# Matrix products of one tile shape put side by side, and the empty rows of the last expert unit left out, in a fused attention and mixture-of-experts kernel

## The chip, the cores and the metric

The kernel runs on 1 core of one Trainium2 chip. The metric is the device time in microseconds, the median of three runs.

## The reference

Eight images of 64 x 64 x 3 and eight texts of 77 tokens of width 64 go through one layer of three parts. In short:

```python
patches = x -> (8, 64 tokens, 192)                  # 8 x 8 patches
t  = ln(ln(patches) @ W1 + b1)                      # to width 64
t  = concat([t, t, t], tokens)                      # three copies: 192 tokens
q  = silu(ln(t @ Wp1 + bp1)) @ Wp2 + bp2
h  = concat([q, txt], tokens)                       # 192 + 77 = 269 tokens
# attention: a linear recurrence over the tokens, state S of 64 x 64 per batch element
r, k, v, w, a, g = ...                              # projections of x and of the shifted x
S  = S * exp(w_t) + (S @ -kk_t) (kk_t a_t)' + v_t k_t' ;  o_t = S @ r_t
h1 = h + (groupnorm(o) + bonus) * g @ W_o
# experts: 8 of them, the best 2 of each token, hidden width 128
c  = softmax over the top 2 of (ln(h1) @ Wg + bg), 0 elsewhere
y  = h1 + sum_e c_e * (relu(ln(h1) @ W1[e] + b1[e]) @ W2[e] + b2[e])
```

## The kernel before

Tokens are cut into chunks of 32. A tile of 128 rows holds 32 tokens of four batch elements (J = 4), and two such groups (G = 2) make the eight. 192 image tokens are 6 chunks, but the three copies share their work, so that there are 6 units to prepare (NU = 6): unit 0 (the first image chunk at the very beginning), 1 and 2 (image), and 3 to 5 (text). Unit 5 (LAST) holds 13 real tokens and 19 empty ones.

**Stages.** First the patches are normalised and projected (`image(i, a)`, two halves a, six sub-steps i). Then the units are prepared in three rounds r with two slots s each (`SLOTS = ((4, 0), (1, 2), (3, 5))`): `proj`, `lora`, `cum`, `hats`, `gates`, `products`, `keep`, `turn`, `apply`, four levels of a doubling inverse (`lt(r, li, s)` and `tlt(r, li, s)`), `out`, `fuse`. `step(k)` and `read(k)` carry the state over the nine chunks. `stats` to `parts` are the norms and the choice of experts, once for each of three groups of three chunks. The expert part has six units of 384 columns (half a group): `front(u, p)` does experts 2p and 2p + 1 (W1 as two rounded parts, L1640 and L1641, and the gate spread over 128 rows, L1652), ScalarE takes the relu (L938) and VectorE multiplies by the gate (L1314). `back(u, p)` adds the same two experts' W2 products (L1674, F32, 64 columns of the array each, the even expert's in rows 0 to 63 of the output and the odd one's in rows 64 to 127), and p = 3 also the b2 term (L1677). ScalarE then copies YS (L947), `fold(u)` adds the two halves of the rows on PE (L1686), VectorE adds the result to H1 (L1328), and SyncE stores it.

**Order.** One function `run` lists all steps. Each engine runs the same list, with its own part of each step (or nothing), in that order; semaphores connect the parts. So a step's place in the list is its place in the queue of all engines that have a part in it.

**Names.** `bank(s, i)` is a PSUM bank of slot s. An F32 product leaves two records in the trace, one in F32R (L1640, L1641, L1652, L1677) one. `residue` is GpSimd's W1l = W1 - W1h (L678), which waits for ScalarE's rounding of W1h in `factors`; `blank` is eight small and two larger memsets on GpSimd (L686 to L690); `remain` is two small subtractions there. The steps on PE, by their lines: `image(0)` L1372, `proj` L1411 (128 x 128), L1414 (128 x 64), L1415 (128 x 128); `cum` L1433 (128 x 128) and L1435 (128 x 64); `products` L1456 (64 x 128); `apply` L1474, L1476 (128 x 128), L1478 (128 x 64), for one g after the other; `lt` L1490; `tlt` L1502, L1506; `out` L1515; `fuse` L1527, L1532 (128 x 64), L1535 (128 x 128); `step` L1557; `read` L1571 (128 x 32).

**Waits that matter below.** `hidden(0)`, the first product of the experts, waits for both `hoc_ready` and `t_ready` of all units, which ScalarE's and VectorE's parts of `fuse(2, 0)` and `fuse(2, 1)` raise. `weights(i, h)` transposes the gate coefficients CP, which VectorE's `parts(i)` completes; ScalarE copies them to CT, on which `spread` waits (`ctc_ready`).

Of the kernel before, what the change touches and what calls it, by code (L numbers as in the profile page):

```python
# [19 lines left out]
F32 = mybir.dt.float32  # L20
# [91 lines left out]
def build(nc, patches, text, consts, pick, rows, cols, tokw, attw, w1, w2, out):  # L112
    ctx = ExitStack()
    with ctx:
# [110 lines left out]
        XHL = [sb(f"XHL{i}", [P, Q, P], F32R) for i in range(GROUPS)]  # L225
        CF = sb("CF", [P, GROUPS * Q, E])
# [17 lines left out]
        CP = sb("CP", [P, Q, 2, E])  # L244
# [105 lines left out]

        NX = E * NU
# [16 lines left out]
        def run(patch=skip, words=skip, even=skip, lift=skip, texts=skip, small=skip, mixes=skip, residue=skip,  # L368
# [48 lines left out]
            lt(0, 2, 0)  # L417
# [3 lines left out]
            tlt(0, 2, 0)  # L421
            keep(0, 1)
            lora(1, 0)
            turn(0, 1)
            lt(0, 3, 0)
            lt(0, 0, 1)
            cum(1, 0)
            tlt(0, 3, 0)
            apply(0, 1)
            out(0, 0)  # L430
            hats(1, 0)
            tlt(0, 0, 1)
            lt(0, 1, 1)
            fuse(0, 0)
            tlt(0, 1, 1)
            proj(1, 1)
            lt(0, 2, 1)
            products(1, 0)
            tlt(0, 2, 1)
            lt(0, 3, 1)  # L440
            keep(1, 0)
            lora(1, 1)
            turn(1, 0)
            tlt(0, 3, 1)
            lt(1, 0, 0)
            gates(1, 0)
            out(0, 1)
            cum(1, 1)
            apply(1, 0)
            fuse(0, 1)  # L450
            tlt(1, 0, 0)
            hats(1, 1)
            gates(1, 1)
            lt(1, 1, 0)
            proj(2, 0)
            products(1, 1)
            tlt(1, 1, 0)
            lt(1, 2, 0)
            lora(2, 0)
            tlt(1, 2, 0)  # L460
            turn(1, 1)
            keep(1, 1)
            cum(2, 0)
            lt(1, 3, 0)
            lt(1, 0, 1)
            apply(1, 1)
            hats(2, 0)
            tlt(1, 3, 0)
            tlt(1, 0, 1)
            lt(1, 1, 1)  # L470
            out(1, 0)
            tlt(1, 1, 1)
            lt(1, 2, 1)
            fuse(1, 0)
# [7 lines left out]
            products(2, 0)  # L482
            keep(2, 0)
            read(1)
            fuse(1, 1)
            turn(2, 0)
            lora(2, 1)
            apply(2, 0)
            step(2)
            cum(2, 1)  # L490
            read(2)
            lt(2, 0, 0)
            step(3)
            stats(0)
            tlt(2, 0, 0)
            read(3)
            centre(0)
            lt(2, 1, 0)
            step(4)
            tlt(2, 1, 0)  # L500
            hats(2, 1)
            gates(2, 1)
            lt(2, 2, 0)
# [3 lines left out]
            tlt(2, 2, 0)  # L507
            keep(2, 1)
            read(5)
# [3 lines left out]
            stats(1)  # L513
            centre(1)
            lt(2, 3, 0)
            lt(2, 0, 1)
            att(0)
            tlt(2, 3, 0)
            tlt(2, 0, 1)
            lt(2, 1, 1)  # L520
            tlt(2, 1, 1)
# [1239 lines left out]
```

## Time and profile before

| | |
|---|---|
| median of 3 runs | 215.8 us (214.55 to 216.31) |
| the profiled execution | 215.78 us, its span 214.0 us |
| mean granted clock | 0.932 of 2.4 GHz |
| busy, of the span | PE 184.4 us (86%), VectorE 149.3 (70%), ScalarE 86.9 (41%), GpSimd 75.6 (35%) |
| instructions | PE 1259, VectorE 539, ScalarE 222, GpSimd 131 |

PE is TensorE's products and PEld its weight loads; DVE is VectorE, ACT ScalarE, POOL GpSimd. Ends of PE's records are modelled and records overlap, so a difference between two starts tells more than a duration. "x4" is four records merged into one row; what stands in brackets is the idle time before a row and what ended it. Of the time outside the span, 1.8 us, the profile shows nothing.

### The profile page before, as it was taken

To read this page: it belongs to the slowest core of one execution; us is meant where nothing else is said; L and a number is where in the kernel's file an instruction comes from. 1 tells how busy PE (TensorE), PEld (TensorE's weight loads), DVE (VectorE), ACT (ScalarE), POOL (GpSimd) and SP (SyncE) were. 2 spreads that over 40 slices of the span, in tenths; PEclk is the share of its full clock that TensorE was granted. 3 is DMA by queue.
4 is the path that set the end of the run, shared out by engine and by line. 5 is a ranking of instruction groups with operands and counts; after the bars stand their busy time and mean duration, and the time that the engine had idled before them with its cause. 6 is when DMAs were issued, how large, how long until landed. Compare 5 with 4: busy or idle time off the path is not lost. (4 is left out here: it accounts for less than half of the span.)

```text
span 214.0 us, 3831 instructions
## 1 busy us (share of the span) xinstructions
PE 184.4 (86%) x1259; PEld 138.9 (65%) x1259; DVE 149.3 (70%) x539; ACT 86.9 (41%) x222; POOL 75.6 (35%) x131
## 2 busy tenths in 40 slices
PE   0584564998999999999999899976899999999994
PEld 0461552586776877977768777854578667866762
DVE  2997658756853884733676989879865978876550
ACT  2062012264454435544323224443464625748440
POOL 3916529653623746514661603273000202000000
PEclk9988555699999999999999999999699999999998
DMA  6920000000000000000000000000000000000000
GB/s 186 335 84 2 0 0 0 0 5 0 2 2 3 0 0 3 0 0 3 0 5 0 0 3 0 2 3 0 0 2 3 0 23 18 0 18 3 18 18 18
DMA packets 2498, 4.06 MB, mean 19 GB/s; under 512 B 416, under 2 KB 1824, under 8 KB 2480
## 3 DMA queue, kind: packets, MB, share of 16 engines
q1 hardware_dynamic: 1872, 3.05, 4.4%
q10 hardware_dynamic: 608, 0.77, 1.1%
q8 instruction: 10, 0.16, 0.3%
q14 instruction: 8, 0.07, 0.1%
HBM read 3.24 MB, written 0.59 MB: 18 GB/s over the span
## 5 line engine op out<-in xcount | busy, mean ns | idle before, releaser
L1171 DVE TENSOR_TENSOR YI<-PS,KC 128x256 f32<-128x256 f32 x24 | 9.8, 419 | 13.1 <-PE PS L1490 12.8
L1640 PE MATMUL PS<-XHL,W1h 128*128 128x384 f32 x48 | 18.4, 383 | 0.0
L783 POOL TENSOR_SCALAR ve<-mv 128x6 f32<-128x6 f32 x6 | 1.5, 258 | 45.3 <-DVE mv L1220 45.3
L1652 PE MATMUL PS<-CT,PK 128*128 128x384 f32 x48 | 16.6, 347 | 0.4 <-ACT CT L929 0.4
L1641 PE MATMUL PS<-XHL,W1l 128*128 128x384 f32 x48 | 16.7, 348 | 0.0
L938 ACT ACTIVATE xT<-PS,CL 128x384 f32<-128x384 f32 x24 | 13.1, 579 | 7.9 <-PE PS L1641 7.7
L1490 PE MATMUL PS<-PI,AT 128*128 128x128 f32 x96 | 15.7, 289 | 0.5 <-DVE BL L1165 0.2
L1506 PE MATMUL PS<-QT,YI 128*128 128x128 f32 x96 | 14.8, 277 | 0.0
L1490 PEld LDWEIGHTS PS<-PI,AT 128*128 128x128 f32 x96 | 12.5, 190 | 2.6 <-ACT PI L883 1.7
L938 ACT ACTIVATE FAB<-PS,CL 128x384 f32<-128x384 f32 x24 | 13.0, 581 | 2.1 <-PE PS L1641 2.1
L1502 PE MATMUL PS<-YI,QT 128*128 128x128 f32 x72 | 12.0, 289 | 1.8 <-DVE YI L1171 1.8
L883 ACT COPY PI<-PS 128x256 f32<-128x256 f32 x18 | 6.7, 373 | 16.6 <-PE PS L1502 16.4
L1506 PEld LDWEIGHTS PS<-QT,YI 128*128 128x128 f32 x96 | 12.7, 192 | 0.1
L1502 PEld LDWEIGHTS PS<-YI,QT 128*128 128x128 f32 x72 | 9.4, 191 | 3.4 <-issue 3.4
L1640 PEld LDWEIGHTS PS<-XHL,W1h 128*128 128x128 f32 x48 | 9.4, 196 | 2.8 <-issue 1.8
L886 ACT COPY QT<-PS 128x256 f32<-128x256 f32 x24 | 8.9, 372 | 3.0 <-PE PS L1506 1.6
L1652 PEld LDWEIGHTS PS<-CT,PK 128*128 128x128 f32 x48 | 9.3, 193 | 0.9 <-issue 0.9
L1342 PE MATMUL PS<-KC,P 128*128 128x128 f32 x13 | 3.4, 334 | 7.4 <-DVE P L974 7.1
L709 POOL TENSOR_TENSOR BL<-BP,KC 128x256 f32<-128x256 f32 x12 | 8.7, 744 | 2.1 <-DVE BP L1126 2.1
L1641 PEld LDWEIGHTS PS<-XHL,W1l 128*128 128x128 f32 x48 | 9.4, 195 | 0.0
L709 POOL TENSOR_TENSOR LKT<-PI,KC 128x256 f32<-128x256 f32 x10 | 7.4, 762 | 5.4 <-ACT PI L895 5.4
L1674 PE MATMUL PS<-HC,W 128*64 128x384 f32 x48 | 9.3, 501 | 0.0
(216 smaller groups left out, 488.2 us busy)
## 6 DMA issues: line engine op xcount, KB each, us to landing
KC<-in_consts SPq DMA_DIRECT2D x1, 706.0 KB, 7.4
out_h<-H SPq DMA_DIRECT2D x6, 96.0 KB, 1.6
ARCH<-in_w SPq DMA_DIRECT2D x1, 512.0 KB, 9.1
AW<-in_attw SPq DMA_DIRECT2D x1, 484.0 KB, 8.3
PT<-in_patches SPq DMA_DIRECT2D x2, 192.0 KB, 3.3
RW<-in_rows ACTq DMA_DIRECT2D x1, 296.0 KB, 5.1
W<-in_w SPq DMA_DIRECT2D x1, 256.0 KB, 9.2
HT<-in_text ACTq DMA_DIRECT2D x1, 192.0 KB, 3.3
```

Source lines behind the costliest of these rows:

```text
L709: return nc.gpsimd.tensor_tensor(dst, src.to_broadcast([P, J, D]), const("block").rearrange("p (j d) -> p j d", j=J), ALU.mult)
L883: copy(PI[s][:, :, :].rearrange("p g t -> p (g t)"), bank(s, 2)[:, 0:G * P])\
L886: copy(QT[s][:, :, :].rearrange("p g t -> p (g t)"), bank(s, 1)[:, 0:G * P]).then_inc(q_ready[s], 1)
L938: nc.scalar.activation(RL[x % len(RL)], PS[:, Z_BANK[x % 2], 0:HALF * P], ACT.Relu, bias=CL[:, COLS["b1e"]][:, e:e + 1]).then_inc(relu_don ...
L1171: TT(YI[s][:, :, :], pairs(bank(s, 2)[:, 0:G * P]), twice(const(f"m{LEVELS[li]}")), ALU.mult)\
L1490: last = mm(bank(s, 2)[:, g * P:(g + 1) * P], AT[s][:, g, :], PI[s][:, g, :], start=True, stop=True)
L1502: last = mm(bank(s, 2)[:, g * P:(g + 1) * P], QT[s][:, g, :], YI[s][:, g, :], start=True, stop=True)
L1506: last = mm(bank(s, 1)[:, g * P:(g + 1) * P], YI[s][:, g, :], QT[s][:, g, :], start=True, stop=True)
L1640: mm(z, W1h[:, e * EH:(e + 1) * EH], xhl, start=True, stop=False)
L1641: mm(z, W1l[:, e * EH:(e + 1) * EH], xhl, start=False, stop=True).then_inc(z_ready, 1)
L1652: mm(PS[:, C_BANK[x % 2], 0:HALF * P], PK[:, e * P:(e + 1) * P], gates_of(u), start=True, stop=True).then_inc(c_ready, 1)
L1674: mm(PS[(e % 2) * D:(e % 2 + 1) * D, Y_BANK, 0:HALF * P], W2[:, e * D:(e + 1) * D], HC[e], start=e < 2, stop=False).then_inc(y_done, 1)
```

## The change

1. `proj`: the product with Wlora's first block writes all 128 columns (64 of A_w and 64 more, which nobody reads) instead of 64. `cum`: the two products per group with `seq` become one with both groups. `apply`: the products with KP (128 x 64) of both groups stand behind the full-width products of both groups.
2. `weights`: CP is 128 wide with zeros behind its 16 coefficients, so its transposes write all 128 rows, and the memsets of CT fall away.
3. The last expert unit (FINAL = 5) has 232 columns: 128 of a full chunk and 2 x 4 x 13 of the last one. `dense` copies its features (XD5) and gates in that form, and its YS is spread again by two copies.
4. `out(2, 1)`, of unit 5 with its 13 tokens, waits for the third level; the fourth, `lt(2, 3, 1)` and `tlt(2, 3, 1)`, leaves the list.
5. The list of `run` gets another order throughout. It has the same steps but for the two of point 4.

```diff
+        FINAL, TAIL = 2 * GROUPS - 1, TXT - (NTXT - 1) * C
+        COUNT = [HALF * P] * FINAL + [P + 2 * J * TAIL]
...
             patch(0)
             patch(1)
             words()
+            texts()
             even(0)
             even(1)
-            texts()
-            lift(0)
-            lift(1)
             small()
             mixes()
             clear()
             factors()
+            lift(0)
+            lift(1)
+            residue()
+            proj(0, 0)
             image(0, 0)
             image(0, 1)
-            proj(0, 0)
-            remain()
-            residue()
+            lora(0, 0)
             image(1, 0)
             image(1, 1)
             image(2, 0)
-            lora(0, 0)
             image(2, 1)
+            blank()
+            cum(0, 0)
+            remain()
             image(3, 0)
             image(3, 1)
             image(4, 0)
-            blank()
-            cum(0, 0)
             image(4, 1)
             hats(0, 0)
             gates(0, 0)
@@ -404,74 +408,74 @@
             products(0, 0)
             keep(0, 0)
             proj(0, 1)
+            apply(0, 0)
             turn(0, 0)
-            apply(0, 0)
             image(5, 1)
+            lora(0, 1)
             lt(0, 0, 0)
-            lora(0, 1)
+            cum(0, 1)
             tlt(0, 0, 0)
-            cum(0, 1)
             lt(0, 1, 0)
...
             heads(1)
             split(0)
-            lt(2, 2, 1)
+            lt(2, 1, 1)
             att(1)
-            tlt(2, 2, 1)
-            lt(2, 3, 1)
+            tlt(2, 1, 1)
             out(2, 0)
             rest(0)
+            lt(2, 2, 1)
             feat(0, 0)
-            tlt(2, 3, 1)
+            tlt(2, 2, 1)
             feat(0, 1)
             split(1)
+            out(2, 1)
             rest(1)
-            out(2, 1)
             rank(0)
-            fuse(2, 0)
             choose(0)
             feat(1, 0)
             feat(1, 1)
+            parts(0)
+            fuse(2, 0)
             fuse(2, 1)
-            parts(0)
             rank(1)
             weights(0, 0)
             front(0, 0)
             weights(0, 1)
+            front(0, 1)
             choose(1)
             parts(1)
-            front(0, 1)
+            back(0, 0)
+            front(0, 2)
             weights(1, 0)
-            front(0, 2)
+            front(0, 3)
             weights(1, 1)
-            front(0, 3)
+            back(0, 1)
             step(6)
-            back(0, 0)
-            back(0, 1)
             back(0, 2)
             read(6)
...
             front(5, 1)
+            back(4, 3)
             front(5, 2)
-            back(4, 3)
+            back(5, 0)
             front(5, 3)
             fold(4)
             tail()
-            back(5, 0)
             back(5, 1)
             back(5, 2)
             back(5, 3)
...
             def clear():
                 nc.gpsimd.memset(PK[:, :].bitcast(F32), 0.0)
-                for s in range(2):
-                    last = nc.gpsimd.memset(CT[s][:, :].bitcast(F32), 0.0)
-                last.then_inc(zeros, 1)
+                nc.gpsimd.memset(CP[:, :, 2:, :], 0.0).then_inc(zeros, 1)
...
+            def dense(dst, src, u):
+
+                if u < FINAL:
+                    return copy(dst, src)
+                copy(dst[:, 0:P], src[:, 0:P])
+                return copy(dst[:, P:COUNT[u]].rearrange("p (q c) -> p q c", c=TAIL),
+                            src[:, P:].rearrange("p (q c) -> p q c", c=C)[:, :, 0:TAIL])
...
+                src = PS[:, FFN_BANK[i], 0:HALF * P]
+                last = copy(XHL[i][:, h * HALF:(h + 1) * HALF, :].rearrange("p q t -> p (q t)"), src)
+                if 2 * i + h == FINAL:
+                    last = dense(XD5[:, :], src, FINAL)
...
-                mm(wide(r, s)[0:D, 0:G * P], Wlora[:, 0:D], x, start=True, stop=True)
+                mm(wide(r, s)[:, 0:G * P], Wlora[:, 0:P], x, start=True, stop=True)
...
                 for i, m in enumerate((masks[:, P:2 * P], masks[:, 0:P], const("suffix"))):
                     mm(bank(s, 0)[:, i * P:(i + 1) * P], m, lw, start=True, stop=True)
-                for g in range(G):
-                    last = mm(bank(s, 0)[g * D:(g + 1) * D, 3 * P:3 * P + J], LW[s][:, g, :], const("seq"),
-                              start=True, stop=True)
-                last.then_inc(cum_ready, 1)
+                mm(bank(s, 0)[:, 3 * P:3 * P + J], lw, const("seq"), start=True, stop=True).then_inc(cum_ready, 1)
...
                        start=True, stop=True)
                     mm(bank(s, 1)[:, P + g * D:P + (g + 1) * D], LKT[s][:, g, 1, :], RK[s][:, g, 2, :],
                        start=True, stop=True)
+                for g in range(G):
                     last = mm(bank(s, 1)[g * D:(g + 1) * D, 2 * P:4 * P], KP[s][:, g, :],
                               VB[s][:, g, :, :].rearrange("p j d -> p (j d)"), start=True, stop=True)
                 last.then_inc(lvov_ready, 1)
...
-                pe.wait_ge(q_ready[s], level(r, 4, 5))
+                pe.wait_ge(q_ready[s], level(r, 3 if SLOTS[r][s] == LAST else 4, 5))
...
-                xhl = XHL[u // 2][:, u % 2 * HALF:(u % 2 + 1) * HALF, :].rearrange("p q t -> p (q t)")
-                z = PS[:, Z_BANK[x % 2], 0:HALF * P]
+                xhl = XD5[:, :] if u == FINAL else XHL[u // 2][:, u % 2 * HALF:(u % 2 + 1) * HALF, :].rearrange("p q t -> p (q t)")
+                z = PS[:, Z_BANK[x % 2], 0:COUNT[u]]
...
```

## Rows read from the trace of the kernel before

**Rows 1.** Windows: stage, its length, busy us and instructions by engine, clock, DMA.

```profile
0.00:42.00 42.00, 23.31 (x91) 16.16 (x91) 29.77 (x120) 9.46 (x25) 24.39 (x53) 0.72 0.23 77
42.00:105.00 63.00, 61.76 (x433) 48.57 (x433) 39.33 (x136) 29.62 (x87) 29.80 (x50) 1.00 0.01 1
105.00:151.00 46.00, 40.09 (x359) 31.84 (x358) 37.67 (x161) 15.15 (x42) 18.19 (x25) 1.00 0.01 1
151.00:155.00 4.00, 3.63 (x14) 2.62 (x12) 3.46 (x12) 2.40 (x7) 0.00 (x0) 0.58 0.00 0
155.00:206.50 51.50, 51.12 (x345) 37.50 (x344) 37.54 (x111) 29.70 (x61) 3.17 (x4) 1.00 0.03 9
```

**Rows 2.** Chain that ended last: start, duration, what (us).

```profile
197.60 2.09 PE PS L1674 x12
199.68 0.37 PE PS L1640
200.06 0.17 PE PS L1641
...
203.94 0.80 PE PS L1674 x4
```

**Rows 3.** PE timeline (start, duration): apply(0, 1), and a fuse of both groups.

```profile
59.96 0.33 PE L1474 MATMUL PS<-RK,LKT 128*128 128x64 f32 x2
...
60.45 0.65 PE L1478 MATMUL PS<-VB,KP 128*64 128x256 f32 x2
61.02 0.43 PE L1474 MATMUL PS<-RK,LKT 128*128 128x64 f32 x2
...
62.19 0.71 PE L1515 MATMUL PS<-LVHA,QT 128*128 128x128 f32 x4
...
65.62 0.60 PE L1532 MATMUL PS<-LKT,BP 128*64 128x256 f32 x4
66.16 0.66 PE L1535 MATMUL PS<-PI,BL 128*128 128x64 f32 x4
```

**Rows 4.** PE timeline: a proj and the step behind it.

```profile
51.59 1.03 PE L1411 MATMUL PS<-Wproj,XT 128*128 128x256 f32 x4
52.55 0.65 PE L1414 MATMUL PS<-XT,Wlora 128*64 128x256 f32 x2
...
53.76 1.13 PE L1456 MATMUL PS<-FAB 64*128 64x256 f32 x8
```

**Rows 5.** PE timeline: the end of cum(1, 1).

```profile
76.55 0.28 PE L1435 MATMUL PS<-KC,LW 128*64 128x4 f32 x4
76.77 0.43 PE L1474 MATMUL PS<-RK,LKT 128*128 128x64 f32 x2
```

**Rows 6.** PE timeline: lt(2, 3, 1) and the step behind it.

```profile
138.14 0.71 PE L1490 MATMUL PS<-PI,AT 128*128 128x128 f32 x4
138.69 0.61 PE L1515 MATMUL PS<-LVHA,QT 128*128 128x128 f32 x4
```

**Rows 7.** PE timeline: the wait ahead of the first weights transposes.

```profile
150.39 0.50 PE L1342 MATMUL PS<-KC,CP 128*16 128x128 f32 x3 [1.95 <-DVE CP L1306]
```

**Rows 8.** Timeline of all engines: two of ScalarE's activations.

```profile
201.99 1.11 ACT L938 ACTIVATE FAB<-PS,CL 128x384 f32<-128x384 f32 x2 [0.61 <-PE PS L1641]
```

**Rows 9.** Timeline of all engines: the cold start.

```profile
11.50 2.00 PE L1372 MATMUL PS<-TW,xT 96*128 96x64 f32 x16
...
14.35 2.04 PE L1411 MATMUL PS<-Wproj,XT 128*128 128x256 f32 x4 [0.85 <-DVE Wproj L1036]
...
19.39 2.84 DVE L974 TENSOR_SCALAR P<-P,mv,rs 128x64 f32<-128x64 f32 x2
...
19.84 2.33 POOL L678 TENSOR_TENSOR W1l<-ARCH,W1h 128x1024 fp32r<-128x1024 f32 x1
...
32.80 1.06 POOL L686 MEMSET ARCH<- 64x256 f32 x4
...
33.80 0.73 POOL L687 MEMSET ARCH<- 64x768 f32 x1
```

More of the change, by code:

```diff
@@ L225, in build @@
         XHL = [sb(f"XHL{i}", [P, Q, P], F32R) for i in range(GROUPS)]
+        XD5 = sb("XD5", [P, P + 2 * J * (TXT - (NTXT - 1) * C)], F32R)
         CF = sb("CF", [P, GROUPS * Q, E])
@@ L243, in build @@
         RC = sb("RC", [P, Q, 1])
[L244 removed]
+        CP = sb("CP", [P, Q, P // E, E])
         CT = two("CT", [P, Q * P], F32R)
@@ L420, in run @@
             products(0, 1)
-            tlt(0, 2, 0)
-            keep(0, 1)
+            lt(0, 2, 0)
             lora(1, 0)
             turn(0, 1)
+            keep(0, 1)
+            tlt(0, 2, 0)
+            cum(1, 0)
             lt(0, 3, 0)
+            apply(0, 1)
+            tlt(0, 3, 0)
             lt(0, 0, 1)
-            cum(1, 0)
-            tlt(0, 3, 0)
-            apply(0, 1)
             out(0, 0)
+            tlt(0, 0, 1)
             hats(1, 0)
-            tlt(0, 0, 1)
             lt(0, 1, 1)
             fuse(0, 0)
+            proj(1, 1)
+            products(1, 0)
             tlt(0, 1, 1)
-            proj(1, 1)
             lt(0, 2, 1)
-            products(1, 0)
-            tlt(0, 2, 1)
-            lt(0, 3, 1)
             keep(1, 0)
             lora(1, 1)
+            tlt(0, 2, 1)
+            gates(1, 0)
             turn(1, 0)
+            apply(1, 0)
+            lt(0, 3, 1)
+            proj(2, 0)
             tlt(0, 3, 1)
             lt(1, 0, 0)
-            gates(1, 0)
             out(0, 1)
+            tlt(1, 0, 0)
+            lt(1, 1, 0)
             cum(1, 1)
-            apply(1, 0)
             fuse(0, 1)
-            tlt(1, 0, 0)
+            tlt(1, 1, 0)
             hats(1, 1)
             gates(1, 1)
[L454 to L457, printed above, removed]
             lt(1, 2, 0)
             lora(2, 0)
+            products(1, 1)
+            keep(1, 1)
             tlt(1, 2, 0)
+            lt(1, 3, 0)
             turn(1, 1)
-            keep(1, 1)
             cum(2, 0)
-            lt(1, 3, 0)
+            apply(1, 1)
+            tlt(1, 3, 0)
             lt(1, 0, 1)
-            apply(1, 1)
+            out(1, 0)
+            tlt(1, 0, 1)
             hats(2, 0)
-            tlt(1, 3, 0)
-            tlt(1, 0, 1)
             lt(1, 1, 1)
-            out(1, 0)
+            fuse(1, 0)
             tlt(1, 1, 1)
             lt(1, 2, 1)
-            fuse(1, 0)
             tlt(1, 2, 1)
@@ L482, in run @@
             products(2, 0)
+            read(1)
             keep(2, 0)
-            read(1)
             fuse(1, 1)
-            turn(2, 0)
             lora(2, 1)
@@ L489, in run @@
             step(2)
+            turn(2, 0)
+            read(2)
             cum(2, 1)
-            read(2)
-            lt(2, 0, 0)
             step(3)
             stats(0)
+            lt(2, 0, 0)
+            read(3)
             tlt(2, 0, 0)
[L496 to L500, printed above, removed]
             hats(2, 1)
             gates(2, 1)
-            lt(2, 2, 0)
+            step(4)
+            lt(2, 1, 0)
+            centre(0)
             read(4)
@@ L506, in run @@
             step(5)
-            tlt(2, 2, 0)
             keep(2, 1)
+            tlt(2, 1, 0)
             read(5)
@@ L567, in run @@
             front(1, 3)
+            back(1, 0)
             centre(2)
-            back(1, 0)
             front(2, 0)
-            fold(0)
             back(1, 1)
@@ L591, in run @@
             rank(2)
-            choose(2)
+            fold(1)
             back(2, 3)
             front(3, 3)
-            parts(2)
-            fold(2)
             back(3, 0)
@@ L599, in run @@
             back(3, 2)
+            choose(2)
+            parts(2)
+            fold(2)
             weights(2, 0)
@@ L946, in back @@
                     act.wait_ge(fin_ready, u)
-                copy(YS[:, :], PS[:, Y_BANK, 0:HALF * P]).then_inc(ys_ready, 1)
+                if u < FINAL:
+                    last = copy(YS[:, :], PS[:, Y_BANK, 0:HALF * P])
+                else:
+                    copy(YS[:, 0:P], PS[:, Y_BANK, 0:P])
+                    last = copy(YS[:, P:].rearrange("p (q c) -> p q c", c=C)[:, :, 0:TAIL],
+                                PS[:, Y_BANK, P:COUNT[u]].rearrange("p (q c) -> p q c", c=TAIL))
+                last.then_inc(ys_ready, 1)
             run(texts=texts, factors=factors, image=image, proj=proj, lora=lora, cum=cum, hats=hats, turn=turn,
@@ L1617, in weights @@
                 else:
+                    pe.wait_ge(zeros, 1)
                     pe.wait_ge(cp_ready, i + 1)
                 for t in range(HALF):
-                    last = transpose(PS[0:2 * E, FFN_BANK[i], t * P:(t + 1) * P],
+                    last = transpose(PS[:, FFN_BANK[i], t * P:(t + 1) * P],
                                      CP[:, h * HALF + t, :, :].rearrange("p w e -> p (w e)"))
```

39 lines of the change are left out of this document (19 added, 20 removed).

## The prediction

> **What bounds the kernel now.** I read the busy table by stage first [rows 1]. It shows TensorE (PE) occupied for 61.76 of 63.0 us between 42 and 105, for 51.12 of 51.5 between 155 and 206.5, at the full clock in both, for 40.09 of 46.0 in between (VectorE, DVE: 37.67), and for only 23.31 of 42.0 in the first stage, where the granted clock averages 0.72 (most of it at 1.2 GHz) and DVE with 29.77 is the busiest engine. "Busy" overstates PE, since its records overlap, so the second view is the chain of work that ended last [rows 2]: from 172 us on, it is one PE product behind the other, with no waits worth naming until the last W2 product. PE takes its steps in one written order. Whatever is taken out of its stream in the two full stages comes off the end; in the first stage a latency chain rules; and between 105 and 151 PE and DVE take turns to be late. The third view is PE's timeline, in which the start of one step is subtracted from the start of the next, for a step's real price.
>
> **What a change of tile shape costs.** A visit of three W2 pairs (128 x 64 tiles) takes 2.08 us, from 197.60 to 199.68, and a visit of one pair 0.80 [rows 2]; so a pair is (2.08 - 0.80) / 2 = 0.64, and 0.16 stays per visit. The first 128 x 128 product behind it takes 0.37 instead of 0.17 to 0.18, 0.20 more [rows 2]. Together 0.36 us per visit, whatever its length. The Trainium skill (TensorEngine Tiling (Array Packing), Key Properties) says that a change of tiling mode drains TensorE, while a change of tile within the mode does not; the trace agrees in kind, and the page has no figure.
>
> **Part 1, apply (6 calls).** Now each group g goes 128 x 128, then 128 x 64: from 59.96 to 61.02 and on to 62.19, 2.23 us [rows 3]. Changed, the narrow products of both groups stand together. The full-width ones cost 0.49 for g = 0 up to the narrow product (59.96 to 60.45) and about 0.44 more for g = 1 without a second entry. The four narrow records write two different halves of the array's columns, as the four of L1532 do, which took 0.54 from 65.62 to 66.16 [rows 3]; with 0.06 for entering cold weights I take 0.60. Sum 1.53, saving 0.70 per call, 4.2 in all: 2.8 before 105, 1.4 behind. The bounds: 0.25 a call, if only the round trip between shapes goes and the two groups don't overlap; 0.75 if they do so perfectly.
>
> **Part 2, proj (6) and cum (6).** Wlora's first product becomes 128 wide and so of the shape of its neighbours. The eight records of 256 columns take 2.17 us, from 51.59 to 53.76 [rows 4]. The first four take 0.96, of which some 0.09 is the entry to the narrow shape, so one is 0.22 and eight are 1.73; with 0.09 for the exit to products' own shape, which stays, 1.82. Saving 0.34, times 5 outside the cold start: 1.7. In cum the four narrow records (0.22 from 76.55 to 76.77, behind an entry of 0.09) [rows 5] become two full-width records. Saving between 0.05 and 0.2 each; I take 0.15, so 0.75 for five.
>
> **Part 3, the last level of unit 5.** lt and tlt of (2, 3, 1) fall away: four records of L1490 and four of L1506. Four take 0.55 with the step to the next (138.14 to 138.69) [rows 6], with some cover between; 0.9 to 1.1 on PE, and one masked copy on DVE. I take 0.95. out(2, 1) then waits for one level less, which can only help.
>
> **What becomes of parts 1 to 3.** Of PE work 2.8 + 4 x 0.34 + 4 x 0.15 = 4.8, with the fifth proj 5.1, lies before 105. DVE is busy 39.33 of 63 there [rows 1], so the stream can close up; but steps that cover each other's copies get shorter while the copies don't, and I take 4.3. The 2.5 behind 105 meet a DVE at 37.67 of 46 that keeps nearly all its work; I take 1.3 (0 to 2.5).
>
> **Part 4, the wait at 150.** PE waits 1.95 us for the gate coefficients CP before the first weights transposes [rows 7]. The new order puts choose(0) and parts(0) ahead of DVE's fuse(2, 0) and fuse(2, 1), so CP is earlier; but hidden(0), the very next product, waits for both of these fuses (t_ready), and DVE does the same sum of work up to there. What is late next is thus t_ready; only the later wait for CT and the dropped masked copy go. Behind the pause the clock fell to half (mean 0.58 over 151 to 155 [rows 1]), where 3.63 busy us would be about 2 us less at full clock. I take 0.5 for all of it (0 to 2.2).
>
> **Part 5, the last unit with 232 columns instead of 384.** Its 24 hidden and spread products would each lose 152 columns / 2.4 GHz = 0.063, 1.5 us. But ScalarE takes 1.11 us for two of its 384-column activations [rows 8], by columns some 0.7 for two of 232 (232/384 of it), so with two banks the fronts can't run at PE's new pace throughout: I take 1.2 (0.8 to 1.5). The four W2 pairs lose 152/384 of 0.64, 1.0 together, and b2's product 0.06. Two copies in place of one for YS stand on the path at the end, 0.1 more. The additional copies into XD5 and CT are ScalarE's, beside products of unit 3: nothing, as long as PE has those; uncovered, 0.5. The net saving of the part is 2.2.
>
> **Part 6, W2 visits.** In the PE order of now, back's steps make 12 visits (those with no other PE step between them count as one); in the new one 15: (0,0), (0,1) and (0,2) stand alone, and so does (5,0). 3 x 0.36 = 1.1 us more, at most 1.1 us less of that where an early visit fills a wait. I take 1.0. The full-width zeros in CP make the transposes write all 128 rows: no column more to stream, and ScalarE's copy has as many columns per row; nothing (0.1 either way).
>
> **Part 7, the cold start.** Two things are traded. W1l's subtraction on GpSimd (POOL) takes 2.33 us from 19.84, and a DVE step on two small tiles takes 2.84 in the same stretch, most of it beside that subtraction; PE and the image chain stand still behind it [rows 9]. It moves ahead of POOL's proj(0, 0), to the moment at which ScalarE has rounded W1h; DVE should then be at lift, which reads PSUM. Against this, even waits behind the text tiles, and image(0) comes behind proj(0, 0) on PE: it now starts at 11.50; behind a proj whose first four of eight records take 2.04 from 14.35 [rows 9], so about 3.9 for all, it starts near 18, 6.5 later. lora(0, 0) comes ahead of image(1, 0) on all queues, and blank's memsets and cum(0, 0) on POOL ahead of image(4)'s root. Against that the text unit, which shared the queues with the image, is out of the way earlier. Stepping it through with the durations of now, I find proj(0, 1), the start of the full stage, within 2 us of where it is, and take 0 (a gain of 2 to a loss of 3.5). The Trainium skill (SBUF — State Buffer, SBUF: two separate sides) states that DVE and GpSimd take a shared pair of ports as an exclusive lock, and that DVE asks for it also with two SBUF inputs against a GpSimd operation that reads SBUF. Both sides of the 2.84 us agree with it. It speaks for the new place as long as lift is there, against it if proj's first sum on DVE (ZA), with two such inputs, falls beside it.
>
> **The sum.** 4.3 + 1.3 + 0.5 + 2.2 - 1.0 + 0 = 7.3. The profiled execution took 215.78, its span 214.0 and 1.8 around it that stays; the median of three is 215.8, so both bases give 208.5 us.
>
> **Rivals.**
> (a) The savings of the middle come back as waits. For: each lt needs ScalarE's PI copy, each tlt DVE's YI copy, and a shorter PE stream covers less of them; DVE is near full from 105 to 151. Against: 24 us of DVE idle time between 42 and 105. With all 5.6 of the middle back: 214.1.
> (b) The change doesn't do what it says in apply: the narrow products of the two groups follow each other instead of overlapping. 6 x 0.45 = 2.7 less: 211.2. Against: L1532's four records in 0.54 [rows 3].
> (c) Slower: the image chain is set back. 6.5 us by proj(0, 0), 1.9 by lora(0, 0) ahead of image(1, 0) (eight records where the sixteen at 11.50 took 2.00, at half the clock), 3.6 by blank ahead of image(4)'s root (memsets of 1.06 and 0.73, each twice [rows 9]), nothing regained but 2.3 of the lock: proj(0, 1), which reads its output, starts 9.7 later, and the sum is 218.2. It decides from 7.3 us of delay on, and is slower by over 1% from 9.5. Against: the image chain has stood behind the text unit's steps in these queues all along, and the new order mostly moves those waits to its beginning.
> (d) Better: the new order also closes waits. From 42 to 151 PE is idle for 1.2 + 5.9 us [rows 1]; if 4 of these go, 204.5.
>
> **How the numbers follow.** Forecast 208.5 with its bounds (205.5 to 211.5): 0.55. (a) 0.15, (b) 0.08, (c) 0.05, (d) 0.17. The range reaches to (d) with a little of its spread and past (b) towards (a): 203.9 to 212.9. 1% (2.2 us) is about what a measurement of this kernel can tell from no change. Faster by more than that: forecast, (b), (d) and a part of (a), 0.85; within it 0.1; slower 0.05.
>
> **What the new profile would show.** Part 1: apply's step at about 1.5 us from first record to the next step's. Part 2: eight records of proj in 1.8. Part 4: the wait before CP's transposes gone and one before hidden(0) in its place. Part 5: unit 5's fronts at 0.4 to 0.45 per expert. Part 6: fifteen times 0.37 behind W2. Part 7: proj(0, 1) at 39 +/- 2 us, and no DVE step on two small tiles over 1 us. The forecast would be wrong most likely by part 7, the only one with a chain instead of a stream, and by the share of parts 1 to 3 that DVE lets through.

## The result and the profile after

The changed kernel took 210.92 us (median of four executions: 213.25, 208.59, 208.52, 213.45) against 216.06 for the kernel before beside it (214.55 to 216.88); the ratio, from the two undisturbed executions of 208.5, is 0.966 (0.957 to 0.975). The profile was taken of the execution of 213.25 us, one with a lower granted clock (0.919) than the two of 208.5 (0.959), and why there are two such kinds is the main subject of what follows. Over three sessions the changed kernel ran 22 times; its times follow the mean granted clock:

| granted clock | executions | us |
|---|---|---|
| 0.959 | 3 | 208.4 to 208.6 |
| 0.951 | 1 | 210.1 |
| 0.939 | 2 | 210.5, 210.7 |
| 0.924 to 0.927 | 5 | 212.6 to 213.5 |
| 0.919, 0.920 | 11 | 213.3 to 214.6 |

So 208.5, the forecast, is what the kernel takes at its best clock, and the median of the 22 is 213.3. The mean orders the executions of this one kernel, not of every one: in the later sessions the kernel before took 212.9 to 213.0 us at 0.943, 214.0 to 214.5 at 0.952, and 216.1 to 216.6 at 0.984. A mean doesn't say where the stretches at half clock lie, so two kernels are compared below by their windows, and by equal means only as a rough second view.

The windows of the kernel after, cut at steps and not at round times: the first product of `proj(0, 1)`, of `step(1)`, of `rank(0)`, `hidden(0)`, and the last b2 product. Columns as in [rows 1].

```profile
39.07:101.52 62.45, 59.67 (x424) 49.74 (x423) 40.94 (x141) 29.76 (x86) 29.32 (x48) 0.98 0.01 1
101.52:138.16 36.64, 31.88 (x314) 26.73 (x313) 29.84 (x139) 12.86 (x37) 15.70 (x23) 1.00 0.00 1
138.16:149.20 11.04, 9.20 (x44) 6.40 (x43) 7.07 (x22) 2.82 (x8) 2.66 (x4) 0.58 0.01 1
149.20:207.26 58.06, 57.20 (x378) 41.17 (x376) 41.16 (x125) 31.77 (x70) 3.17 (x4) 0.96 0.03 9
```

The same cuts in the kernel before:

```profile
39.05:104.07 65.02, 63.78 (x433) 49.18 (x431) 41.20 (x141) 29.55 (x86) 31.12 (x51) 0.98 0.01 1
104.07:142.60 38.53, 35.33 (x325) 28.55 (x323) 30.98 (x141) 13.26 (x38) 15.94 (x23) 1.00 0.01 2
142.60:150.64 8.04, 5.33 (x41) 3.87 (x42) 7.17 (x22) 2.55 (x8) 2.70 (x4) 1.00 0.00 0
150.64:209.66 59.02, 58.27 (x379) 41.78 (x376) 42.46 (x125) 32.20 (x67) 3.17 (x4) 0.97 0.03 9
```

Stage by stage, before less after: start -0.02, then 2.57, 1.89, **-3.00**, 0.96, and 0.12 from the last b2 product to the end of the span: 2.52 in all, which is 215.78 - 213.25 but for 0.01. One short stage, from `rank(0)` to `hidden(0)`, gives 3.0 us back, and it is the one in which the clock stands at 0.58. The busy columns show it at once: DVE's work there is the same (7.17 and 7.07), PE's went from 5.33 to 9.20 for three records more.

The records of the clock have it fall at 139.99 and rise at 153.64. Windows cut there, the 5 us before the fall and the stretch at half clock:

```profile
139.99:153.64 13.65, 12.70 (x49) 9.37 (x49) 9.16 (x28) 4.68 (x12) 1.45 (x2) 0.50 0.00 1
135.00:139.99 4.99, 3.11 (x25) 2.84 (x26) 3.47 (x9) 2.44 (x6) 4.08 (x5) 1.00 0.00 0
```

PE is busy for 3.11 of the 4.99 us ahead of the fall. PE's timeline of the place, in the kernel after:

```profile
135.71 0.52 PE L1360 MATMUL PS<-KC,XD 128*128 128x128 f32 x3 [0.96 <-DVE XD L1286]
...
139.93 0.83 PE L1360 MATMUL PS<-KC,XD 128*128 128x128 f32 x3 [0.95 <-DVE XD L1286]
141.65 0.90 PE L1360 MATMUL PS<-KC,XD 128*128 128x128 f32 x3 [0.89 <-ACT XHL L924]
...
143.82 1.07 PE L1548 MATMUL PS<-LKT,BP 128*64 128x256 f32 x4
144.82 1.12 PE L1551 MATMUL PS<-PI,BL 128*128 128x64 f32 x4
...
148.65 0.90 PE L1360 MATMUL PS<-KC,CP 128*128 128x128 f32 x3
149.20 0.67 PE L1657 MATMUL PS<-XHL,W1h 128*128 128x384 f32 x1
```

The wait of 1.95 us for CP [rows 7] is gone: nothing stands in brackets at 148.65. Beside the wait at 135.71 stand two at the transposes of `feat(1, 0)` and `feat(1, 1)`, since the products of `fuse(2, 0)`, which used to lie ahead of these, now come behind both. The first of the two is new. The second stood in the kernel before too, as in the row below, and that at 135.71 also (1.01 us, at 140.30):

```profile
146.31 0.55 PE L1342 MATMUL PS<-KC,XD 128*128 128x128 f32 x3 [0.76 <-ACT XHL L915]
```

So the waits of the stage are shorter than before, 0.95 and 0.89 where there were 0.76 and 1.95, and still it is longer.

The slow clock shows in `fuse`: L1548 goes at 1.00 from 143.82 to 144.82, where a fuse at full clock took 0.54 for its four records of this form [rows 3]. And DVE, which has CP ready early (L1323, at 143.92), now waits for PE (DVE's timeline):

```profile
146.04 0.59 DVE L1203 TENSOR_TENSOR ARCH<-PS,FAB 64x128 f32<-64x128 f32 x2 [1.91 <-PE PS L1551]
```

### The profile page after: what moved, and what is told of

Same layout as the page of the kernel before. It is cut to its first block and busy times, and to the rows that moved or that the text cites. A ratio compares the mean times of both kernels' runs of the same rounds, so it can differ in the third digit from the quotient of the medians.

```text
span 211.4 us, 3795 instructions
## 1 busy us (share of the span) xinstructions
PE 177.4 (84%) x1239; PEld 138.8 (66%) x1239; DVE 146.6 (69%) x538; ACT 86.6 (41%) x225; POOL 75.7 (36%) x130
## 5 line engine op out<-in xcount | busy, mean ns | idle before, releaser
L1669 PE MATMUL PS<-CT,PK 128*128 128x384 f32 (+1 forms) x48 | 16.3, 339 | 0.1
L1657 PE MATMUL PS<-XHL,W1h 128*128 128x384 f32 x40 | 15.8, 396 | 0.0
L949 ACT ACTIVATE xT<-PS,CL 128x384 f32<-128x384 f32 (+1 forms) x24 | 12.6, 562 | 7.8 <-PE PS L1658 7.8
L1506 PE MATMUL PS<-PI,AT 128*128 128x128 f32 x92 | 15.0, 288 | 0.2
L1658 PE MATMUL PS<-XHL,W1l 128*128 128x384 f32 x40 | 14.2, 354 | 0.0
L949 ACT ACTIVATE FAB<-PS,CL 128x384 f32<-128x384 f32 (+1 forms) x24 | 12.5, 561 | 2.4 <-PE PS L1658 2.4
L1360 PE MATMUL PS<-KC,XHD 128*128 128x128 f32 x10 | 2.6, 403 | 11.2 <-DVE XHD L1000 11.2
L1657 PEld LDWEIGHTS PS<-XHL,W1h 128*128 128x128 f32 x40 | 8.1, 203 | 2.3 <-issue 1.2
L1360 PEld LDWEIGHTS PS<-KC,XHD 128*128 128x128 f32 x10 | 1.6, 200 | 11.7 <-issue 10.2
L1691 PE MATMUL PS<-HC,W 128*64 128x384 f32 (+1 forms) x48 | 9.2, 484 | 0.0
```

The costliest lines, as they stand in the source:

```text
L949: nc.scalar.activation(RL[x % len(RL)][:, 0:n], PS[:, Z_BANK[x % 2], 0:n], ACT.Relu, bias=CL[:, COLS["b1e"]][:, e:e + 1]).then_inc(relu_do ...
L1360: return nc.tensor.transpose(dst, src, ident)
L1506: last = mm(bank(s, 2)[:, g * P:(g + 1) * P], AT[s][:, g, :], PI[s][:, g, :], start=True, stop=True)
L1657: mm(z, W1h[:, e * EH:(e + 1) * EH], xhl, start=True, stop=False)
L1658: mm(z, W1l[:, e * EH:(e + 1) * EH], xhl, start=False, stop=True).then_inc(z_ready, 1)
L1669: mm(PS[:, C_BANK[x % 2], 0:COUNT[u]], PK[:, e * P:(e + 1) * P], gates_of(u), start=True, stop=True).then_inc(c_ready, 1)
```

## Experiments

**First: which part gives what, and does the time repeat?** The changed kernel again, and three kernels that hold part of the change. One chip, kernel before 215.76 us (214.0 to 216.9, 17 executions).

The changed kernel, unchanged (e_after):

> The changed kernel again, for its two levels (208.5 and 213.4 us so far) and a trace of the lower one. Clock theory: the whole distance is the stretch at half clock behind the waits around 140, 13.65 us long in the profiled execution of 213.25; an execution near 208.5 has at most one stretch of 3.4 us there, and the same instructions with the same waits before 138 us. Rival: the levels differ at the cold start, proj(0, 1) beginning over 2 us earlier in the lower one.

Measured: 213.21 us (210.47 to 214.56, 12 executions), ratio 0.986 (0.981 to 0.991); not one reached the clock of 0.959, and with it none 208.5. The first result's gain isn't the usual one. The profiled execution (214.35 us at 0.920) is again one of the low level, with the same 13.65 us at half clock, so that no trace of the high level came of it and the expectation stays untested here.

All edits of the code, the steps in the order of before without `lt(2, 3, 1)` and `tlt(2, 3, 1)`:

```diff
# the list of run: the lines of the kernel before, less
-            lt(2, 3, 1)
-            tlt(2, 3, 1)
```

> All edits of the code, with the list of run as it was before (only lt(2, 3, 1) and tlt(2, 3, 1) taken out). Price theory (shapes 5.6 in the middle, last unit 2.2, no new W2 visits): 215.8 - 7.8 - 0.5 = 207.5, so the new order is worth nothing or costs 1. Rival (the order is what pays, the shapes alone come back as waits): 212 to 214.

Measured: 212.37 us (212.06 to 212.62), ratio 0.987 (0.981 to 0.993): 4.9 over the 207.5 expected. All four executions have a mean clock of 0.918 or 0.919.

The kernel before with the tile shapes of `proj`, `cum` and `apply` alone:

```diff
-                mm(wide(r, s)[0:D, 0:G * P], Wlora[:, 0:D], x, start=True, stop=True)
+                mm(wide(r, s)[:, 0:G * P], Wlora[:, 0:P], x, start=True, stop=True)
...
-                for g in range(G):
-                    last = mm(bank(s, 0)[g * D:(g + 1) * D, 3 * P:3 * P + J], LW[s][:, g, :], const("seq"),
+                mm(bank(s, 0)[:, 3 * P:3 * P + J], lw, const("seq"), start=True, stop=True).then_inc(cum_ready, 1)
...
+                for g in range(G):
                     last = mm(bank(s, 1)[g * D:(g + 1) * D, 2 * P:4 * P], KP[s][:, g, :],
```

> The kernel before with only the three edits of tile shape: proj's wide product, cum's single one, apply's narrow products of both groups together. Price theory: 6 x 0.70 + 5 x 0.34 + 5 x 0.15 = 6.6 us of PE stream, of which 4 to 6 arrive: 210 to 212. Rival (waits take it back): 214 or more.

Measured: 212.48 us (211.80 to 212.75), ratio 0.988 (0.981 to 0.995), 0.5 above the upper end of 210 to 212.

The kernel before with the rest of the code's edits (232 columns, wide CP, the level left out; old shapes, old order):

```diff
+        COUNT = [HALF * P] * FINAL + [P + 2 * J * TAIL]
...
+                nc.gpsimd.memset(CP[:, :, 2:, :], 0.0).then_inc(zeros, 1)
...
+                pe.wait_ge(q_ready[s], level(r, 3 if SLOTS[r][s] == LAST else 4, 5))
```

> The kernel before with only the last unit's 232 columns, the wide CP transposes and the dropped level of unit 5; shapes and order as before. Price theory: 2.2 from the unit and 0.5 from the level: 213.1. Rival (ScalarE and VectorE bound the fronts of the last unit, nothing arrives from it but the W2 products): 214.5.

Measured: 213.64 us (211.46 to 215.26), ratio 0.990 (0.982 to 0.997). The windows of these kernels tell more than their times. First stage of e_shapes, first stage of e_old_order, last stage of e_padding:

```profile
39.26:100.28 61.02, 59.12 (x424) 49.63 (x423) 42.57 (x141) 29.91 (x88) 31.33 (x51) 0.98 0.01 1
```

```profile
40.23:101.32 61.09, 59.32 (x425) 49.79 (x423) 42.55 (x141) 29.98 (x88) 31.14 (x51) 0.97 0.01 1
```

```profile
152.37:209.29 56.92, 56.23 (x378) 41.43 (x376) 40.82 (x124) 31.47 (x70) 3.18 (x4) 0.97 0.03 10
```

The shapes alone take 65.02 to 61.02, 4.0 us; with the old order this stays, with the new one it is 62.45. The padding takes 59.02 to 56.92, 2.1 us, at the same clock. Each stage gives what was expected of it, but the sum doesn't arrive: e_old_order too stood at half clock, from 138.9 for 13.65 us. Its window from `rank(0)` to `hidden(0)`:

```profile
139.18:149.39 10.21, 9.64 (x41) 6.99 (x42) 7.52 (x23) 2.87 (x8) 3.16 (x5) 0.50 0.00 0
```

So the long stretch at half clock comes with the order of before as well, once all edits of the code are in; with the shapes alone it was 6.8 us (from 144.26), with the padding alone 3.41 (from 152.2), in one profile each. And with this stretch in both, the new order is the slower one: from `proj(0, 1)` to the last b2 product 168.19 us in the changed kernel and 166.25 in e_old_order, and 213.3 to 214.6 against 212.1 to 212.6 in whole executions at 0.918 to 0.920. That made the granted clock the suspect, and the new order's waits ahead of `step(1)` the second.

**Second: is it the clock?** If PE is kept busy where it waits, with products whose result nobody reads, and the time falls by what the slow products cost, it was the clock. Nothing else is changed: idle 128-column products into the unused end of bank 0.

```diff
+            def warm(n, b):
+                for _ in range(n):
+                    mm(PS[:, b, 3 * P:4 * P], ident, ident, start=True, stop=True)
...
+            warm(4, 0)
             feat(0, 0)
...
+            warm(5, 0)
             feat(1, 0)
+            warm(3, 0)
             feat(1, 1)
...
+            warm(4, 0)
             front(0, 0)
```

> The changed kernel with 16 idle products (F32, 128 columns, into a PSUM bank that nobody reads then) on PE, put where it waits between the chunks of the expert choice: 4 before feat(0, 0), 5 before feat(1, 0), 3 before feat(1, 1), 4 before front(0, 0). They compute nothing that is used. Clock theory: the clock stays at its upper level from 41 us to the end, fuse(2, 0) and fuse(2, 1) take 2.6 us on PE instead of 4.9, hidden(0) comes 3 us earlier, the experts start at the full clock (2 us more): 208.5 in every execution, where the changed kernel has 210.5 to 214.5 on this chip. Rival (VectorE's chain through rank, choose and the fuses sets hidden(0), whatever PE's clock): 212 to 214, and the fillers only add.

Measured: 209.06 us (208.43 to 209.38, 6 executions), ratio 0.968 (0.964 to 0.972). The two lines of the page that show the granted clock in 40 slices, after and e_warm:

```profile
PEclk9999555699999999999999999975599999999999
```

```profile
PEclk9999855599999999999999999999999999999999
```

The windows of e_warm, at the same four cuts:

```profile
38.84:101.43 62.59, 59.58 (x424) 49.89 (x423) 41.17 (x141) 29.78 (x86) 29.36 (x48) 0.98 0.01 1
101.43:138.07 36.64, 32.78 (x323) 27.63 (x321) 29.83 (x139) 12.88 (x37) 15.70 (x23) 1.00 0.01 2
138.07:146.56 8.49, 8.02 (x68) 6.68 (x67) 7.12 (x22) 2.82 (x8) 2.61 (x4) 1.00 0.00 0
146.56:203.34 56.78, 55.46 (x379) 39.69 (x377) 41.11 (x125) 31.63 (x70) 3.17 (x4) 1.00 0.03 9
```

Sixteen more products (32 records of L1703 in the trace) on the busiest engine, and the kernel is faster and steady. The first two stages are the same to 0.14; 11.04 became 8.49 and 58.06 became 56.78, 3.8 us together. The Trainium skill (TensorE: Matmul & The Clock Gate, Part 1) says that a block watches how busy PE has been and gates its clock by it; this pair of runs agrees.

**Third: are fewer W2 visits better, and the old order up to step(1)?** In the same session (kernel before 216.33, 214.36 to 217.02) the changed kernel with 12 visits:

```diff
-            back(0, 0)
...
-            back(0, 1)
             step(6)
+            back(0, 0)
+            back(0, 1)
             back(0, 2)
...
-            back(5, 0)
...
             tail()
+            back(5, 0)
             back(5, 1)
```

> The changed kernel with W2 in the 12 visits of before: back(0, 0) and back(0, 1) behind step(6), back(5, 0) behind tail. Price theory: 3 x 0.36 = 1.0 us less than the changed kernel on the same chip, read between hidden(0) and the last b2 product (58.1 to 57.1). Rival (the early visits fill waits and cost nothing): no change.

Measured: 214.61 us (211.45 to 216.44), ratio 0.986 (0.977 to 0.995). At like clocks it is 1.1 to 1.6 slower than the changed kernel (214.19 at 0.928 against 212.6 to 213.1 at 0.927; 211.45 at 0.949 against 210.09 at 0.951), and from `hidden(0)` to the last b2 product it takes 59.63 us (150.82 to 210.45), not 57.1 as expected nor 58.06 as in the changed kernel.

The list of before up to `step(1)`, the new list behind it with 12 visits; without and with the 16 idle products:

```diff
# e_mix: the list up to step(1) from the kernel before, the rest as in e_visits12
# e_mix_warm: the same and warm(...) as in e_warm
```

> The changed kernel with the list of before up to step(1) (as long as that list has the same steps), the new one behind, and W2 in the 12 visits of before. Stage table theory: the new order costs 1.5 us between proj(0, 1) and step(1) and its three W2 visits 1.0, so this gains 2.5 on the changed kernel: 210.7 with the long stretch at half clock, 206 without. Rival (the two halves of the list fit each other only as they are): 213 or more.

Measured: 211.96 us (211.55 to 216.53), ratio 0.981 (0.975 to 0.987). Four of the five lie at 0.942 or 0.943, by their mean without the long stretch at half clock, where 206 was expected; the fifth (216.53 at 0.912), which was profiled, has it.

> e_mix with the same 16 idle products. Clock theory and stage table theory together: 206.0 in every execution, below both kernels. Rival as for e_warm: 210.7.

Measured: 211.04 us (210.81 to 212.09), ratio 0.978 (0.973 to 0.984), 5.0 over what was expected. First and last window of e_mix_warm:

```profile
38.84:100.25 61.41, 59.45 (x424) 49.91 (x423) 42.58 (x141) 29.90 (x88) 31.34 (x51) 0.97 0.01 1
...
147.04:205.22 58.18, 55.06 (x378) 39.81 (x376) 41.09 (x125) 31.60 (x70) 3.17 (x4) 1.00 0.03 10
```

61.41 instead of 62.59: the old order is better ahead of `step(1)`. But 58.18 instead of 56.78 with three visits fewer, PE busy for 55.06 and not 55.46. PE's busy time fell by 0.4, and the rest of the stage, in which PE stands, grew from 1.3 to 3.1 us; two of the waits in e_mix_warm are this one for CP and 0.66 us for CT at 155.26:

```profile
152.71 0.52 PE L1364 MATMUL PS<-KC,CP 128*128 128x128 f32 x3 [0.91 <-DVE CP L1327]
```

Where `back(0, 0)` and `back(0, 1)` stood, PE now waits for the gates of the next unit.

**Fourth: the parts at one clock.** One chip, kernel before 215.98 us (212.94 to 217.17, 23 executions). The changed kernel once more (e_again):

> The changed kernel once more, beside the next three on one chip. If the granted clock is what spreads its times, it gives 208.5 to 214.5 us and each time goes with its clock: 208.5 at 0.959, 210.5 at 0.939, 213.4 at 0.920. If the chip is what spreads them, times at one clock differ by more than 1 us.

Measured: 213.82 us (208.39 to 214.60), ratio 0.974 (0.961 to 0.986). 208.39 at 0.959, 210.09 at 0.951, the other four at 0.919 or 0.920 with 213.5 to 214.6: one chip gives both ends, so it isn't the chip.

The changed kernel with apply's old loop:

```diff
-                for g in range(G):
                     last = mm(bank(s, 1)[g * D:(g + 1) * D, 2 * P:4 * P], KP[s][:, g, :],
```

> The changed kernel with apply as before, one group behind the other (six calls). Theory (0.70 per call, four of them ahead of step(1) in a full stream): proj(0, 1) to step(1) 2.5 to 2.9 us longer than in the changed kernel, 65.2 instead of 62.45, and 2.2 to 4 us more in all at the same granted clock. Rival (the new order's waits already hold this time, so that shorter products only wait longer): 1 us or less ahead of step(1).

Measured: 214.06 us (212.56 to 218.22), ratio 0.994 (0.989 to 1.000), no gain left. Against the changed kernel at like clocks: 212.6 to 213.0 against 208.4 to 208.6 at 0.96; 214.0 to 214.6 against 210.1 at 0.95; 218.2 against 213.3 to 214.6 at 0.92. So about 4.2, six times 0.70. The medians on this chip show nothing of it (214.06, and 213.82 for e_again): two of the ten executions fell to the low clock (0.921) with the old loop, four of six without it. Its windows:

```profile
39.79:104.81 65.02, 62.41 (x424) 50.94 (x423) 40.51 (x141) 29.79 (x86) 29.30 (x48) 0.98 0.01 1
104.81:142.88 38.07, 33.31 (x314) 27.25 (x313) 29.85 (x139) 12.86 (x37) 15.69 (x23) 1.00 0.01 1
142.88:151.04 8.16, 5.69 (x45) 4.03 (x43) 6.81 (x21) 2.82 (x8) 2.62 (x4) 1.00 0.01 2
```

2.57 in the first stage for four calls and 1.43 in the second for two. The third row is of use too: this profiled execution kept its clock without idle products, with the changed order, and there the stage takes 8.16. Its waits are at the same places, and no shorter:

```profile
144.65 0.52 PE L1360 MATMUL PS<-KC,XD 128*128 128x128 f32 x3 [0.95 <-DVE XD L1286]
146.38 0.55 PE L1360 MATMUL PS<-KC,XD 128*128 128x128 f32 x3 [1.21 <-ACT XHL L924]
```

The kernel before with the same 16 idle products:

```diff
# the kernel before, and warm(...) as in e_warm
```

> The kernel before with the same 16 idle products at the same steps (ahead of feat(0, 0), feat(1, 0), feat(1, 1) and front(0, 0)) and nothing else. Theory (before loses only its 3.41 us at half clock behind 150.9, about 1.5 us of work, and pays for the idle products where PE does not wait): 215.0 us (214.0 to 216.2), so that at one clock the change is worth about 6 us. Rival (idle products alone are what makes e_warm fast): 211 us or less.

Measured: 214.14 us (212.66 to 216.82, 12 executions), ratio 0.996 (0.991 to 1.000): 2 us of gain at most, so idle products alone are not what makes e_warm fast. Windows:

```profile
37.68:102.38 64.70, 63.46 (x432) 49.07 (x431) 41.09 (x141) 29.56 (x86) 31.25 (x51) 0.98 0.01 1
102.38:140.92 38.54, 36.22 (x332) 29.44 (x331) 31.00 (x141) 13.26 (x38) 15.93 (x23) 1.00 0.01 2
140.92:149.59 8.67, 7.96 (x65) 6.64 (x66) 7.76 (x25) 2.66 (x8) 2.71 (x4) 1.00 0.00 0
149.59:207.73 58.14, 56.90 (x379) 40.84 (x377) 41.63 (x122) 32.18 (x67) 3.17 (x4) 1.00 0.03 10
```

From `proj(0, 1)` to the last b2 product that is 170.05, and 164.50 in e_warm: at full clock throughout, **the change is worth 5.55 us behind the cold start**. That is one profile of each; in whole executions e_warm is 5.1 us faster (209.06 against 214.14), and without idle products the one changed execution at 0.951 (210.09) is some 4.3 below the kernel before at 0.952 (214.0 to 214.5).

Last, what the runs pointed to: the old list up to `step(1)`, the new one with its 15 visits behind it, the idle products and 4 more ahead of `tlt(2, 0, 0)`, where e_mix_warm had lost its clock for 3.41 us.

```diff
# the list up to step(1) from the kernel before, the rest and warm(...) as in e_warm, and
+            warm(4, 0)
             tlt(2, 0, 0)
```

> All edits of the code; the list of the kernel before up to step(1), the new list (with its 15 visits) behind it; the same 16 idle products as in e_warm and 4 more ahead of tlt(2, 0, 0). Theory (the new order costs 1.1 to 1.5 us ahead of step(1), and its 15 visits are no loss behind it): 1.1 below e_warm's 209.06, 208.0 us, hidden(0) to the last b2 product in 56.8. Rival (what the new order loses ahead of step(1) it gives back behind it in any case, since VectorE is ahead when PE is late): 209 us, with step(1) to rank(0) at 37.9 instead of 36.6.

Measured: 208.92 us (208.01 to 209.56), ratio 0.972 (0.966 to 0.978). First two windows:

```profile
40.01:100.84 60.83, 58.98 (x424) 49.64 (x423) 42.37 (x141) 29.92 (x88) 31.17 (x51) 0.98 0.01 1
100.84:137.55 36.71, 33.93 (x328) 28.67 (x329) 30.20 (x140) 12.53 (x36) 15.73 (x23) 1.00 0.01 2
```

The rival falls in its mechanism (36.71, not 37.9: the new order behind `step(1)` doesn't need the late start), yet holds in the number. 1.76 us are saved up to `step(1)`, and 1.17 of them go ahead of it, where `proj(0, 1)` began at 40.01 and not at 38.84. e_best and e_warm beat both kernels and can't be told apart by their times.

## Why the prediction came out as it did

The number, the sign and the range held for the first four executions. But 208.5 was hit by the kernel at its best clock only, with two errors that cancel there, and the median of all 22 (213.3) lies 0.4 above the range. Point by point:

**Part 1, apply: right.** PE's timeline of apply(0, 1) after, L1489 and L1491 being the products of L1474 and L1476 in [rows 3]:

```profile
58.48 0.33 PE L1489 MATMUL PS<-RK,LKT 128*128 128x64 f32 x2
...
59.42 0.65 PE L1494 MATMUL PS<-VB,KP 128*64 128x256 f32 x4
60.00 0.38 PE L1522 MATMUL PS<-QT,YI 128*128 128x128 f32 x1
```

1.52 us from 58.48 to 60.00, forecast 1.53; the four narrow records take 0.58 (0.60). Rival (b) falls: the narrow products of the two groups do overlap. e_apply_per_g puts the part at 4.2 us of time, as forecast.

**Part 2, proj and cum: right.** A proj and the step behind it, then cum's end, in the kernel after:

```profile
51.20 1.03 PE L1429 MATMUL PS<-Wproj,XT 128*128 128x256 f32 x4
52.07 0.59 PE L1432 MATMUL PS<-XT,Wlora 128*128 128x256 f32 x2
...
53.02 1.13 PE L1471 MATMUL PS<-FAB 64*128 64x256 f32 x8
...
57.81 0.28 PE L1452 MATMUL PS<-KC,LW 128*128 128x4 f32 x2
57.95 0.69 PE L1506 MATMUL PS<-PI,AT 128*128 128x128 f32 x4
```

The eight records take 1.82 (forecast 1.82; 2.17 in [rows 4]); cum's end takes 0.14 where it took 0.22 behind an entry [rows 5].

**What becomes of parts 1 to 3: right for the edits, wrong for the order.** Forecast 4.3 ahead of 105 and 1.3 behind. The shapes alone gave 4.0, but the new order takes 1.4 of it (1.8 by e_best against e_warm), so 2.6 remained. The first of its waits is one that the old order doesn't have, because `cum(0, 1)` now stands ahead of `tlt(0, 0, 0)`:

```profile
46.37 0.91 PE L1451 MATMUL PS<-LW,KC 128*128 128x128 f32 x6 [0.78 <-DVE LW L1109]
```

Behind `step(1)` the order pays: 38.20 with the shapes alone, 37.86 with all edits in the old order, 36.64 in the new. 1.9 instead of 1.3, so 4.5 in all against 5.6. Of rival (a), that the savings come back as waits, a fifth is true; of rival (d), that the order closes waits, 1.2 us, in one stage.

**Part 4, the wait at 150: the step that failed.** It was right that the wait for CP would go and that something else is late next. It was wrong in what: in the kernel after `hidden(0)` starts without a wait, and the waits of the stage are those for the copies XD and XHL at the transposes of the two halves, 0.95 and 0.89 us. The forecast wait for `t_ready` shows only at full clock, and is short: in e_apply_per_g PE stands for 0.31 us ahead of `hidden(0)`, up to 0.1 us behind the end of DVE's last sum of `fuse(2, 1)`, which raises `t_ready` (the profile names no releaser there):

```profile
150.35 0.59 DVE L1203 TENSOR_TENSOR ARCH<-PS,FAB 64x128 f32<-64x128 f32 x2
...
151.04 0.41 PE L1656 MATMUL PS<-XHL,W1h 128*128 128x384 f32 x1 [0.31 <-issue]
```

With the clock kept, the stage takes 8.16 against 8.04: nothing gained where 0.5 was forecast. The step took a low clock behind the pause for something that can only get better. What the runs showed in its place: before, the clock fell behind the long wait at the end of the thin stretch, for 3.41 us, which cost 0.9 (59.02 against 58.14) and not the "about 2 us" of the prediction; now it falls at the beginning of that stretch, at 139.99 (in 16 of the 22 executions, by their mean clocks of 0.927 and below), and 13.65 us at half speed cover `fuse`, `rank`, `weights` and the first experts. The new places of the waits alone don't explain this, since e_old_order fell as early and as long; why the clock falls so much earlier is not shown. The price is 11.04 - 8.16 = 2.9 us ahead of `hidden(0)` and 58.06 - 57.10 = 1.0 behind it by e_apply_per_g, 2.55 and 58.06 - 56.78 = 1.3 by e_warm, which also spends time on its idle products: 3.8 us by either. e_apply_per_g's own times agree, 214.1 at 0.952 and 218.2 at 0.921. The range of the step went from 0 to 2.2 gained; it should have gone to 4 lost.

**Part 5, the last unit: right.** 2.1 measured (e_padding) of 2.2. Its fronts and its last visit in the kernel after:

```profile
203.31 0.28 PE L1657 MATMUL PS<-XD,W1h 128*128 128x232 f32 x1
203.43 0.27 PE L1658 MATMUL PS<-XD,W1l 128*128 128x232 f32 x1
203.54 0.27 PE L1669 MATMUL PS<-CT,PK 128*128 128x232 f32 x1
203.75 0.61 PE L1691 MATMUL PS<-HC,W 128*64 128x232 f32 x4
204.29 0.38 PE L1657 MATMUL PS<-XD,W1h 128*128 128x232 f32 x1
204.50 0.27 PE L1658 MATMUL PS<-XD,W1l 128*128 128x232 f32 x1
```

A product each 0.11, so 0.33 per expert: PE keeps its own pace, not ScalarE's (0.4 to 0.45 was forecast), though ScalarE takes 0.80 for the two activations, not 0.7. These go beside the W2 visit.

**Part 6, the visits: the price right, its place half so.** The first product behind a visit is 0.21 from the next (204.29 to 204.50) where the others are 0.11 apart, and the visit of one pair takes 0.54: entry and exit cost what [rows 2] said. In e_before_warm less the padding's 2.1 the last stage would be 56.0, and it is 56.78 in e_warm: some 0.7 lost, by this subtraction, of the 1.0. But the three visits are no fault: without them the stage takes 58.18.

**Part 7, the cold start: right, by compensation.** `proj(0, 1)` starts at 39.07 (39.05 before). Over all profiled executions the eight with the old beginning start it at 37.7 to 40.2 (mean 39.43), the six with the new one at 38.8 to 40.0 (mean 39.45). Rival (c) falls: `image(0)` started at 16.30, not near 18, for `proj(0, 0)` took 1.83 there and not 3.9: it ran at full clock, and the 2.04 of [rows 9], from which the 3.9 came, at half. No DVE step on two small tiles took over 1 us; what DVE did beside W1l's subtraction (15.19 to 17.54) was ZA, which took 1.44 us and 0.29 before, where it didn't stand beside it: the case that the prediction named as speaking against the new place.

**The two errors that cancel.** At full clock behind the start the change is worth 5.55 us by the windows, not 7.3: by the cuts it gave 2.1 (forecast 4.3), 1.9 (1.3), 0.2 (0.5) and 1.4 (1.2). That makes 210.2; the rest of the way to 208.5 is in part clock that the profiled execution of before hadn't got: it stood at half clock for 3.41 us behind 150.92, worth 0.9 of its last stage (59.02 against 58.14), and its mean is 0.932 where those of 208.5 have 0.959. Some 0.8 is left; how much of it is the start wasn't measured, since no execution of 208.5 has a profile.

## What to carry to other kernels

Products of one tile shape side by side were worth their full price here, in the full stage and in the one in which PE waits: six regroupings of 0.70 gave 4.0 us by the windows and 4.2 by times at like clocks. Before taking products out of a stretch where PE is thin, or moving waits about in it, ask what the granted clock may do there: in this kernel the stretch at half clock grew from 3.41 to 13.65 us, with either order, and sixteen idle products in the waits were worth more than the reorder. And compare two kernels stage by stage and in many executions: four executions said 5.1 us of gain, and the median of 22 lies 2.5 to 3.0 us below the medians of the kernel before. Last, count what a step costs together with what it fills: three W2 visits priced at 1.0 us stood where there were 1.8 us of waits without them.

## What the hardware showed that was not expected

- The clock stood at half for 3.41 us (before, from 150.92) or 13.65 us (after, from 139.99), between one stretch of products and the next with gaps of at most 1 us in the 5 us ahead of the later fall. It isn't the same each time: the 0.95 and 1.21 us gaps of e_apply_per_g, in a profiled execution, brought no fall, and two kernels with the same list up to there differed by a 3.41 us stretch at 115 (e_visits12 had it, and 38.18 from `step(1)` to `rank(0)` for 36.64). What decides between them stays open.
- Sixteen idle products of 128 columns made six executions lie within 1 us, where the same kernel without them spread over 6.
- In the cold start one and the same order gives 37.7 to 40.2 us for the same step, with 17.07 or 20.48 us at half clock; e_warm with 17.07 began the full stage at 38.84, e_best with 20.48 at 40.01.
